# Order of the three partial products in the units by tokens of a graph and expert layer

## What is computed

```python
xn = layernorm(x)
h  = relu(xn @ W_self0 + mean(xn) @ W_neigh0 + b0)
gnn = h @ W_self1 + mean(h) @ W_neigh1 + b1
q, k, v = xn @ Wq, xn @ Wk, xn @ Wv           # 16 heads of 64
attn = softmax(q) @ (softmax(k).T @ v)        # per head
x = x + gnn + attn @ Wo + bo
y = layernorm(x)                              # top 2 of 8 experts per token
routed = sum(w_e * (silu(y @ w1[e]) @ w2[e]))
shared = sigmoid(y @ gate_w) * ((silu(y @ gate) * (y @ up)) @ down)
x = x + routed + shared
```

## Time and profile before

| | us |
|---|---|
| median of three runs | 1040.83 |
| lowest and highest | 1040.35, 1041.01 |
| the profiled execution | 1040.68 |
| its span, first to last instruction | 1038.9 |
| PE busy in matmuls | 1022.6, x6224 |
| DVE busy | 658.4 |
| ACT busy | 460.2 |
| POOL busy | 79.2 |

### The profile page before, as it was taken

The page is one execution under the profiler, slowest core; times in us unless marked ns, Lnnn a source line. Parts: engine busy times, 40 slices in busy tenths (PEclk is TensorE's granted clock), DMA queues, the critical chain, the costliest instruction groups (busy, mean ns, idle before and its releaser), DMA issues.

```text
span 1038.9 us, 16292 instructions
## 1 busy us (share of the span) xinstructions
PE 1022.6 (98%) x6224; PEld 914.7 (88%) x6224; DVE 658.4 (63%) x970; ACT 460.2 (44%) x731; POOL 79.2 (8%) x123
## 2 busy tenths in 40 slices
PE   7999999999999999999999999999999999999998
PEld 5889998787888899987878899998989999998977
DVE  6789968666655765234337365124878787787846
ACT  4423344557777622221122342212666575567630
POOL 6000010000000000000000007000101000010103
PEclk9999999999999999999999999999999999999999
DMA  9821112033212221262200524233789677688918
GB/s 354 313 82 51 73 41 82 7 113 125 82 61 82 82 81 35 106 222 81 81 1 1 180 83 110 87 117 139 253 303 353 236 264 266 229 269 301 343 39 298
DMA packets 76694, 156.44 MB, mean 151 GB/s; under 512 B 8489, under 2 KB 8987, under 8 KB 76618
## 3 DMA queue, kind: packets, MB, share of 16 engines
q1 hardware_dynamic: 65656, 127.30, 35.7%
q0 software_dynamic: 6416, 20.00, 5.4%
q10 hardware_dynamic: 4546, 8.10, 2.1%
HBM read 133.89 MB, written 21.49 MB: 150 GB/s over the span
## 4 chain that ended last, share of the span: by engine, by line
PE 86%; DVE 4%; ACT 4%; DMA 2%; DVEq 2%; issue 1%; POOL 1%; ACTq 0%; POOLq 0%; SPq 0%
PE ps L1988 19%; PE ps L1990 19%; PE ps L1989 19%; PE ps L2452 7%; PE ps L2477 6%; PE ps L2453 3%; PE ps L2478 2%; PE ps L2087 1%; PE ps L2319 1%; PE ps L2250 1%; PE ps L2320 1%; PE ps L2251 1%; PE ps L2101 1%; PE ps L2034 1%; DMA y_second<-expert_rows,slots 1%
## 5 line engine op out<-in xcount | busy, mean ns | idle before, releaser
L1199 DVE TENSOR_TENSOR w_lo<-w_raw,w_hi 128x2048 fp32r<-128x2048 f32 x41 | 93.1, 2288 | 38.8 <-ACT w_hi L801 36.7
L2452 PE MATMUL ps<-xe,w_hi 128*128 128x304 f32 (+2 forms) x384 | 107.3, 357 | 0.0
L1988 PE MATMUL ps<-w_hi,xt_hi 128*128 128x512 f32 (+1 forms) x240 | 96.0, 400 | 3.5 <-DVEq L1509 2.0
L801 ACT CAST w_hi<-w_raw 128x2048 fp32r<-128x2048 f32 x41 | 77.1, 1908 | 45.2 <-PE ps L2320 36.2
L2453 PE MATMUL ps<-xe,w_lo 128*128 128x152 f32 (+2 forms) x384 | 94.4, 246 | 0.0
L1990 PE MATMUL ps<-w_hi,xt_lo 128*128 128x512 f32 (+1 forms) x240 | 93.6, 390 | 0.0
L1989 PE MATMUL ps<-w_lo,xt_hi 128*128 128x512 f32 (+1 forms) x240 | 93.6, 390 | 0.0
L1193 DVE TENSOR_TENSOR w_lo<-w_raw,w_hi 128x1024 fp32r<-128x1024 f32 x68 | 79.8, 1221 | 13.7 <-ACT w_hi L797 11.7
L2477 PE MATMUL ps<-he,w_hi 128*128 128x304 f32 (+1 forms) x320 | 88.2, 355 | 0.0
L797 ACT CAST w_hi<-w_late 128x1024 fp32r<-128x1024 f32 x64 | 63.0, 1053 | 45.0 <-PE ps L1990 18.4
L1193 DVE TENSOR_TENSOR w_lo<-w_late,w_hi 128x1024 fp32r<-128x1024 f32 x64 | 75.2, 1221 | 7.5 <-ACT w_hi L797 4.8
(11 more groups left out here) (371 smaller groups left out, 2355.0 us busy)
## 6 DMA issues: line engine op xcount, KB each, us to landing
w_raw<-in_L_ffn_w SPq DMA_DIRECT2D x64, 512.0 KB, 5.7
w_late<-in_L_ffn_w SPq DMA_DIRECT2D x64, 512.0 KB, 5.1
w_raw<-in_L_gnn_W_neigh SPq DMA_DIRECT2D x8, 1024.0 KB, 6.0
w_raw<-in_L_gnn_W_self SPq DMA_DIRECT2D x8, 1024.0 KB, 5.1
w_raw<-in_L_ffn_shared_gate_up SPq DMA_DIRECT2D x8, 1024.0 KB, 6.0
expert_rows<-ctx_s POOLq DMA_DIRECT2D x15, 512.0 KB, 13.4
w_raw<-in_L_mix_Wv SPq DMA_DIRECT2D x4, 1024.0 KB, 14.8
w_raw<-in_L_mix_Wk SPq DMA_DIRECT2D x4, 1024.0 KB, 5.7
```

The lines of the kernel that those rows point to most:

```text
L801: copy(w_hi[b][:, s * HK:(s + 1) * HK, :], w_raw[s][:, :, :]).then_inc(hi_done, 1)
L1199: V_.tensor_tensor(w_lo[b][:, k, :], w_raw[s][:, :, :], as32(w_hi[b][:, k, :]), ALU.subtract).then_inc(lo_done, 1)
L1988: mat(out_ap, lh, rh, start=start, stop=False)
L2452: mat(PS(key)[:, a, 0:2 * width], wh[:, k, w_cols], xe[:, :, k, 0:width], start=k == 0, stop=False)
```

## The change

The three products of a row group are no longer made one after another. The unit first makes the hi by hi product of all eight row groups, with the waits that stood ahead of each row group; then hi by the weights' lo part for all eight, then lo by hi for all eight. The number of matmuls, their operands and the accumulator are the same; `mat` is `nc.tensor.matmul`.

```diff
--- before.py
+++ after.py
@@ -2010,8 +2010,10 @@
                         pe.wait_ge(lo_out, arrives(k))
                     if comes:
                         comes(k)
-                    last = passes(out_ap, [t[:, k, tokens] for t in operand], (wh[:, k, :], wl[:, k, :]),
-                                  start and k == 0, stop and k == KF - 1)
+                    mat(out_ap, operand[0][:, k, tokens], wh[:, k, :], start=start and k == 0, stop=False)
+                for row, w in ((operand[0], wl), (operand[1], wh)):
+                    for k in range(KF):
+                        last = mat(out_ap, row[:, k, tokens], w[:, k, :], start=False, stop=stop and k == KF - 1 and w is wh)
                 return last
```

## The result

| | us |
|---|---|
| before, median of five runs beside it | 1040.35 |
| changed, median of five runs | 1049.64 |
| changed, all five | 1049.17, 1049.38, 1049.64, 1049.85, 1051.65 |
| ratio, with its 95% interval | 1.0092 (1.0081 to 1.0103) |
| the profiled execution of the changed kernel (the longest of the five), its span | 1051.65, 1049.9 |

1048.6 was forecast, with 1045.9 to 1051.3.

What follows compares the result with a forecast made beforehand. The prediction took TensorE's matmuls, busy 1022.6 of 1038.9 us, to bound the kernel. Pace 0 plus stalls of 2.16 + 1.22 + 3.20 + 1.23 = 7.81 us on the median 1040.83 gave 1048.6, range 1045.9 to 1051.3.

Steps and rivals of the forecast that it cites:

- The pace: All 1704 matmuls of 512 columns: stays 0.227 us each, so the change costs 0, within 1.7 us either way.
- The stalls: Five units by tokens where PE reaches a row group before its lo part is written: 7.81 us in sum.
- first g1: First g1 unit: row group 7 waits for the lo part of the last h unit; stall 2.16 us.
- sd (0, 0): First shared output unit: its eighth matmul waits for the last up unit's lo part; stall 1.22 us.
- y (1, 0, 0), y (6, 0, 0): First output units of the experts with one tile: row group 4 waits for ht 1's lo part; 1.60 us each.
- y (7, 0, 0): Looped expert, once: row group 6 waits for the lo part of he 3; stall 1.23 us.
- Waits on weights: Expert 1, hu 1 and y (1, 1, 0): weight pieces arrive before they are needed; cost 0.
- The tail: Stores, gathers and last additions after the last expert: shifts as a whole with the end of its y units.
- Rival A: Later PE waits on `lo_of` shrink, giving back 1.8 us: 1046.8 us; chance 0.06.
- C: Runs of eight from one weight tile stream at 213 ns a matmul, 23.9 us less: 1024.7 us; chance 0.03.
- D: PE can work past the new waits, so the change does nothing: 1040.8 us; chance 0.03.
- Rival B: TensorE's clock falls after new stalls, 1.9 us each; 1058.1 us if all five; chance 0.05 for one to five falls.

Runs made afterwards that it cites:

- e1: Against the changed kernel: new order in the 66 units by tokens without an arrives wait, old order in the five that have one; 1040.54 us, ratio 1.0000.
- e2: Against the changed kernel: new order only in the first output units of the two experts with one tile, old order elsewhere; 1044.67 us, ratio 1.0043.
- e7: Changed kernel with matmuls that compute nothing used filling all five stalls; 1048.47 us, ratio 1.0074.
- e3: Changed kernel with five unused matmuls filling the stall in each first output unit of the two experts with one tile; 1049.52 us, ratio 1.0097.
- e4: Changed kernel with waits where operands are read: first pass waits for the hi part, third pass for the lo part; 1042.65 us, ratio 1.0017.
- e5: Against the changed kernel: old order in the first output units of the two experts with one tile, new order elsewhere; 1046.19 us, ratio 1.0054.
- e6: Against the changed kernel: two products per row group, waiting for hi only, then lo by hi for all eight, waiting for lo; 1040.67 us, ratio 1.0000.

## Why the prediction was right, and what it missed

**The pace.** 0 with bounds of 1.7 us; e1 measured 0.1 by PE's last matmul, and as a time nothing within its interval of 0.9 us. Right, and for the reason given: the steps of the earlier trace rows are equal whether the stationary tile repeats or not.

**The stalls.** Forecast against the length of each unit in the changed kernel or, for the experts with one tile, in e2:

| unit | forecast | measured |
|---|---|---|
| first g1 | 2.16 | 7.59 - 5.51 = 2.08 |
| sd (0, 0) | 1.22 | 6.67 - 5.46 = 1.21 |
| y (1, 0, 0), y (6, 0, 0) | 1.60 each | 1.55, 1.56 |
| y (7, 0, 0) | 1.23 | 6.81 - 5.56 = 1.25 |
| sum | 7.81 | 7.65 |

e7 has 7.8 as a time, e3 7.69 by PE's last matmul. What was read is where each lo part ends on DVE and where its row group would come, and that held to 0.1 us a unit. The 0.11 us from DVE's end to PE's start was a little long for four of the five stalls: in the changed kernel ht 1 ended at 778.03 + 0.69 = 778.72 and PE went on at 778.77, 0.05 later, and for h 7, up 7 and expert 6 it is 0.06. For he 3 it is 0.12.

```profile
778.03 0.69 DVE L1205 TENSOR_TENSOR he<-ps,he 128x512 fp32r<-128x512 f32 x1
```

The 0.11 came from a wait that, as e4 showed, was one for the slot.

**Waits on weights** were hidden as forecast: no new one stands in the list above. **The tail** shifted as a whole in the changed kernel's profile: the first shared output after the loop is added from 1023.29 on instead of 1012.44, 10.85 later, as PE's last matmul. But its length is a spread that the prediction had put at nothing. Between PE's last matmul and the end DVE works off its additions, some of which wait for gathered rows. Its last one, in the kernel before, in e3 and in e7:

```profile
1036.04 0.48 DVE L1945 SCALAR_TENSOR_TENSOR x<-ps,wts,x 113x256 f32<-113x256 f32 x1 [0.20 <-issue]
...
1044.87 0.48 DVE L1945 SCALAR_TENSOR_TENSOR x<-ps,wts,x 113x256 f32<-113x256 f32 x1 [0.20 <-issue]
...
1042.82 0.48 DVE L1945 SCALAR_TENSOR_TENSOR x<-ps,wts,x 113x256 f32<-113x256 f32 x1 [0.20 <-issue]
```

It starts 1.9, 3.1 and 1.2 us after PE's last matmul. So single executions of e3 and e7, 1049.52 and 1047.46 as profiled, differ by 2 us where their PE differs by 0.2. To compare stalls and falls, PE's last matmul and the lengths of the units are the better measure; a single time carries about 1 us of this either way.

**Rival A, given back later,** is out: the three waits on L1207 are still 1.8 us. **C**, a faster stream, fell with e1, **D** with the list of waits.

**Rival B, the clock,** had 0.05 and is the part that was missed. It had been set up as an alternative, with the forecast taken to be free of falls. By the sign that the prediction named, a granted clock that falls in these stretches, B is right for two of its five stalls in the profiled execution. Its size was near: 1.9 us a fall, measured 1.6. (That 1.9 was read from durations alone: over 4 to 8 and 8 to 12 us the windows of the kernel before show a granted clock of 1.00, so they don't bear out the fall at the start that the durations of the earlier trace rows show.) But the reason for holding B low was not good. I had said that the new stalls, up to 2 us, were nearer to the 0.71 us ahead of y (1, 0, 0), after which the clock held, than to the 4.99 at the start; in truth that left it open, as no row lay between. With one fall in the likely case the forecast would have been 1048.6 + 1.6 = 1050.2 beside 1040.83 before, and the measured ratio on it gives 1050.4. The range held because one fall fits in it, and that is partly luck: the profiled execution, with two, took 1051.65 and lies outside.

The section HAM oscillation — how this bites in real kernels, of the Trainium skill's page "TensorE: Matmul & The Clock Gate", was named beside that rival: waits between batches of matmuls can lower the clock. The runs agree that idle time is the cause: with the same stalls filled with matmuls (e7) the mean clock is 0.999 or above in five executions, where the changed kernel has 0.998 or less in each of five. The kernel of that section waits longer between its batches than any stall here; that waits of 0.71 and 1.28 us can be enough is what these windows add.

**What stays open.** Which idle time brings a fall in a given execution. In one and the same profile 1.81 us passed at full clock, while 0.71 and 1.28 us with transposes just ahead of them did not; in e2's profile 0.72 and 1.26 us passed at full clock as well. e5 shows that some other stall can do it too, but its executions with a lower clock weren't the profiled one, so which of the three it was isn't known.

## What to carry to other kernels

In a chain of matmuls over hi and lo parts, put each wait ahead of the product that reads its operand: all three regroupings make the product with the late lo part last, but with its wait left ahead of the first pass the change costs 0.9%, and with the wait at its reader 0.17% (e4). Then see how early each row group is reached: with two products per row group ahead of the last pass the hi parts are in time too and nothing is lost (e6). Before such a regrouping list the units with a wait inside, and for each compare the end of the operand's write with the start of the matmul that will now need it; units without a wait can be passed over (e1). For a stall on TensorE reckon with more than its length: here each fall of the clock after one cost another 1.6 us.

## What the runs showed of the hardware

- In the changed kernel, idle times of 0.71 and 1.28 us with four matmuls between them, after small transposes, were followed by a fall of the granted clock from 1.00 to 0.50 (2.4 to 1.2 GHz) from 779.5 to 782.5 us; eight matmuls of 512 columns then took 3.20 us instead of 2.00. It isn't the same in every execution: in e2's profile idle times of 0.72 and 1.26 us in the same unit left the clock at 1.00.
- Loading the same stationary tile twice in a row is neither cheaper nor dearer than loading a new one, at 512 columns: 0.12 us over 1584 matmuls.
- After a stall the second matmul starts 0.34 us after the first instead of 0.23 (442.34 to 442.68): the restart costs 0.11 us beside the wait here, and 0.13 over four matmuls in the earlier trace rows.
